# A perceiver kernel: who adds up the exponentials of the second attention

## The chip, the cores and the metric

One core of one Trainium2 chip runs the whole program in one launch. The time is device microseconds of that core, the median of several runs. Five engines work side by side, each with an instruction queue of its own: TensorE (PE in the profile, with its weight loads as PEld), VectorE (DVE), ScalarE (ACT), GpSimd (POOL) and the queue that issues most DMAs (SP). They wait for one another through semaphores only.

## The reference

The program is two layers on 512 latent rows of 512 numbers: a cross attention against 8192 context rows, a scan, experts, a second cross attention against the same context, a linear attention, and a causal attention with experts. The second cross attention, of 16 heads of 32 numbers, is the one that is touched. With q, k and v made before it:

```
for each head h:                       # q: 512 x 32, k and v: 8192 x 32
    s   = (q_h @ k_h.T) * scale        # 512 x 8192
    e   = exp(s - rowmax(s))
    att = (e @ v_h) / e.sum(-1)        # the divisor is the "den" of the names below
out = x + concat(att) @ Wo.T + bo
```

Everything is float32.

## The kernel before

`cross_attention` (L563) serves both cross attentions; `masked` tells the first (with a mask) from the second. The 8192 keys of a head are 64 blocks of 128 keys, taken as 32 pairs, here called steps 0 to 31. A block's scores lie transposed, 128 keys by 512 queries, in a bank of PSUM, so that a sum over keys is a sum over partitions and over tiles.

What each engine issues in a step is fixed by its own loop over `g` (head and step):

- TensorE: `scores` of the first block (L746), `maxima` (L708, two matmuls that give the scores of a later head, 36 steps ahead, for its row maxima), `scores` of the second block, and at every even step a `wave` (L757): the exponentials of four blocks times v, four matmuls in four column groups of 32. Each f32 matmul of a wave runs in two passes, so a wave shows as 8 matmul records. At step 18 (`OUT_STEP`) comes `head_out` of the head before (L783 to L787), at step 29 four small transposes of the maxima (L727).
- ScalarE: two exponentials per step (L861), from PSUM into one of 16 tiles `prob` of 128 x 2 x 512 (two of them lie in the tensor `xnT`), written again 16 steps later, once `tile_free` says that both the wave and the sum are done with the tile.
- VectorE: one `reduce_max` per step over two banks (L927), which frees those banks for the `maxima` two steps on; at step 19 `den_sum` (L967, L969), at step 27 `top_of_rows` (L941), at step 30 `m_lo_rows` (L946). In heads 4, 8 and 12 it also has eight reciprocals (L973), one each at steps 20 to 27.
- GpSimd: adds most `prob` tiles into `den_pool` (L1039 for the first two, L1045 for the others, 128 x 1024 each), and issues the DMAs that add some of the tiles into `den_dma` (L1027, L1031). At step 3 it issues `merge`, a DMA that adds `den_dma` of the head before into `den_pool` (L1021).

The class `Sums` says who sums which tile. Before, in heads 0 to 14 of the second attention: TensorE takes waves 9, 10 and 11, which are tiles 18 to 23, by multiplying them with a matrix of ones (`sum_wave`, L770, four matmuls per wave, issued right behind the wave, into a bank of their own); DMAs take tiles 2, 5, 8, 11, 14, 17, 24, 27 and 30; GpSimd takes the other 17. ScalarE then copies the bank into `den_pe` (`take_sums`, L880), and `head_out` sums `den_pe` over partitions with a matmul of ones (L783). Head 15 has a list of its own (waves 9 to 15 on TensorE).

`Banks` plans the PSUM banks. Three of them (0, 1 and 7) go round between the blocks of scores; "out" (the result of `head_out`) takes one of the three for some steps, and "sums" takes one from step 20 until after step 24, so that the blocks have two left. TensorE may write a block once ScalarE has read the block that was in its bank.

The first attention gives its first five tiles of each head to VectorE, in whole tiles (L957, L960), and GpSimd's first add of the head waits for them.

Of the kernel before, what the change touches and what calls it, by code (L numbers as in the profile page):

```python
# [5 lines left out]
F32 = mybir.dt.float32  # L6
# [4 lines left out]
ALU = mybir.AluOpType  # L11
# [3 lines left out]
P = 128  # L15
T = 512
# [4 lines left out]
H = 16  # L21
DH = D // H
# [395 lines left out]
PAIRS = KT // 2  # L418
# [8 lines left out]
def wave_step(w):  # L427

    return 2 * w + 2
# [39 lines left out]
class Sums:  # L469
# [1 line left out]

    def __init__(self, by_dve, waves, by_dma, last_waves, last_by_dma):
        self.by_dve, self.waves, self.last_waves = by_dve, waves, last_waves
        self.dma_tiles, self.last_dma_tiles = by_dma, last_by_dma
        self.dve_adds = max(0, len(by_dve) - 1)
        self.first_two = 0 if by_dve else 1
        self.pool_adds = len(self.by_pool(0)) - self.first_two

    def pe_waves(self, h):
        return self.waves if h + 1 < H else self.last_waves

    def by_dma(self, h):
        return self.dma_tiles if h + 1 < H else self.last_dma_tiles

    def by_pool(self, h):
        return [p for p in range(PAIRS) if p not in self.by_dve and p not in self.by_dma(h) and p // 2 not in self.pe_waves(h)]

    def pe_done(self, h, w):  # L490

        return len(self.waves) * h + self.pe_waves(h).index(w) + 1

    def dma_done(self, h, p, n_dma):

# [67 lines left out]
def cross_attention(k, ctx, q_hi_lo, k_hi_lo, v_heads, wo, w_out, x_rows, comb, scale, masks, attT):  # L563
# [8 lines left out]
    n_q, n_p = 3, 7 if masked else 16  # L572
    kring = 22 if masked else 36
    if masked:
        sums = Sums([0, 1, 2, 3, 4], [], list(range(5, PAIRS - 2, 3)), [12, 13, 14, 15], [5, 8, 11, 14, 17, 20, 23])
    else:
        sums = Sums([], [9, 10, 11], [2, 5, 8, 11, 14, 17, 24, 27, 30], [9, 10, 11, 12, 13, 14, 15], [2, 5, 8, 11, 14, 17])
    banks = Banks((0, 1, 7), 7, sums)
    q_stack = [k.sbuf(ctx, "q_stack", [QROWS + 2, T], F32R) for _ in range(n_q)]
    k_ring = k.sbuf(ctx, "k_ring", [QROWS + 2, kring, KC], F32R)  # L580
# [9 lines left out]
    den_pe = prob[(PAIRS * (H - 1) + 24) % n_p][:, 0, :] if not sums.waves else k.sbuf(ctx, "den_pe", [P, T], F32)[:]  # L590
# [10 lines left out]
    s_top, s_topT, s_mhi, s_mlo = k.sem("s_top"), k.sem("s_top_turned"), k.sem("s_m_hi"), k.sem("s_m_lo")  # L601
    s_score, s_exp, s_wave = k.sem("s_score"), k.sem("s_exp"), k.sem("s_wave")
    s_pre = k.sem("s_mask_first")
    s_ddve, s_dpool, s_dsum = k.sem("s_den_dve"), k.sem("s_den_pool"), k.sem("s_den_sum")
    s_ddma = [k.sem("s_den_dma", keep=True) for _ in range(n_dma)]
    s_merge = k.sem("s_den_merged", keep=True)
# [11 lines left out]
    def bank_of(kind, n):  # L618
        return k.bank(banks.bank[kind, n])

    def pe_sums(h):

        return h + 1 if sums.waves else int(h + 1 == H)

    def wait_for_bank(e, kind, n):

        if banks.user_before[kind, n] is None:
            return
        kind, n = banks.user_before[kind, n]
        if kind == "block":  # L630
            e.wait_ge(s_exp, n + 1)
        elif kind == "out":
            e.wait_ge(s_dsum, n + 1)
        elif kind == "sums":
            e.wait_ge(s_pesum, pe_sums(n))
        else:
            e.wait_ge(s_mlo, n + 1)

# [8 lines left out]
    with nc.Block() as block:  # L647
# [47 lines left out]
        def _(e):  # L695
# [79 lines left out]
            def head_out(h):  # L775

                out = bank_of("out", h)
                e.wait_ge(s_osb, h + 1)
                wait_for_bank(e, "out", h)
                e.wait_ge(s_merge, 16 * (h + 1))  # L780
                if sums.pe_waves(h):
                    e.wait_ge(s_pesum, pe_sums(h))
# [53 lines left out]
        @block.scalar  # L836
        def _(e):
            def m_hi_rows(h):
                e.wait_ge(s_topT, h + 1)
                e.activation(q_stack[h % n_q][rows_m, :], bank_of("rows", h)[rows_m, :], ACT.Copy).then_inc(s_mhi, 1)  # L840

            def tile_free(g):

                if g < n_p:
                    return
                e.wait_ge(s_wave, waves_done(g - n_p))
                h, p = divmod(g - n_p, PAIRS)
                if p // 2 in sums.pe_waves(h):
                    e.wait_ge(s_sumw, sums.pe_done(h, p // 2))
                elif p in sums.by_dve:  # L850
                    e.wait_ge(s_ddve, sums.dve_done(h, p))
                elif p in sums.by_dma(h):
                    e.wait_ge(s_ddma[h % n_dma], 16 * sums.dma_done(h, p, n_dma))
                else:
                    e.wait_ge(s_dpool, sums.pool_done(h, p))

            def exponentials(b):
                e.wait_ge(s_score, b + 1)
                if b % 2 == 0:
                    tile_free(b // 2)  # L860
                e.activation(prob[b // 2 % n_p][:, b % 2, :], bank_of("block", b), ACT.Exp, scale=scale  # L861
                             ).then_inc(s_exp, 1)

            def mask_first(b):

                wait_for_bank(e, "block", b)
                e.activation(bank_of("block", b), masks[1][:, b % KT, :], ACT.Copy, scale=BIG).then_inc(s_pre, 1)  # L867

            def take_values(h):
                e.wait_ge(s_wave, WAVES * (h + 1))  # L870
                if h > 0:
                    e.wait_ge(s_head, h)
                e.activation(o_sb[:], vbank, ACT.Copy).then_inc(s_osb, 1)

            def take_sums(h):

                if h > 0:
                    e.wait_ge(s_head, h)
                e.wait_ge(s_sumw, sums.pe_done(h, sums.pe_waves(h)[-1]))
                e.activation(den_pe, bank_of("sums", h), ACT.Copy, scale=1.0 / DH).then_inc(s_pesum, 1)  # L880

            def head_rows(h):
                g = slice(DH * (h % 4), DH * (h % 4) + DH)
                e.wait_ge(s_head, h + 1)
                out = bank_of("out", h)
                e.activation(attT[g, h // 4, :], out[0:DH, :], ACT.Copy).then_inc(s_att, 1)
                if h % 4 == 0 and h > 0:
                    e.wait_ge(s_div, h // 4)
                e.activation(den4[g, :], out[DH:2 * DH, :], ACT.Copy).then_inc(s_att, 1)

            if masked:
                for q in range(PAIRS):
                    c2, i = divmod(q, TT)
                    a = turned_banks(q)[0]
                    e.wait_ge(s_maskT, q + 1)
                    e.activation(masks[0][:, i, 2 * c2 * KC:2 * (c2 + 1) * KC],
                                 k.psum[:, a:a + 2, :].rearrange("p b n -> p (b n)"), ACT.Copy).then_inc(s_maskq, 1)
            m_hi_rows(0)
            for g in range(H * PAIRS):
                h, p = divmod(g, PAIRS)  # L900
                exponentials(2 * g)
                if masked and g % 2 == 0:
                    mask_first(2 * g + 2)
                if p == wave_step(WAVES - 1) - PAIRS + 1 and h > 0:
                    take_values(h - 1)
                if p == PAIRS - 2 and h + 1 < H:
                    m_hi_rows(h + 1)
                exponentials(2 * g + 1)
                if p == OUT_STEP and h > 0:
                    head_rows(h - 1)  # L910
                if h + 1 < H and sums.waves and p == wave_step(sums.waves[-1]):
                    take_sums(h)
            take_values(H - 1)
            take_sums(H - 1)
            head_rows(H - 1)

        @block.vector
        def _(e):
# [30 lines left out]
            def add_tile(h, j):  # L949
# [8 lines left out]
                else:  # L958
                    e.wait_ge(s_ddve, sums.dve_adds * h + j)
                    e.tensor_tensor(den[:], den[:], tile, ALU.add).then_inc(s_ddve, 1)  # L960

            def den_sum(h):
                g = slice(DH * (h % 4), DH * (h % 4) + DH)
                e.wait_ge(s_att, 2 * h + 2)
                out = bank_of("out", h)
                if sums.pe_waves(h):
                    e.tensor_tensor(den4[g, :], den4[g, :], out[3 * DH:4 * DH, :], ALU.add).then_inc(s_dhalf, 1)  # L967
                    e.wait_ge(s_dhalf, pe_sums(h))
# [13 lines left out]
            for g in range(H * PAIRS):  # L982
# [2264 lines left out]
```

## Time and profile before

| | |
|---|---|
| median of 3 runs | 4158.3 us (4152.01 to 4160.54) |
| span of the profiled execution | 4154.8 us |
| TensorE busy | 3803.5 us, 92% |
| VectorE busy | 2806.4 us, 68% |
| ScalarE busy | 2342.3 us, 56% |
| GpSimd busy | 1867.7 us, 45% |
| first exponential of the second attention | 2452.5 us |
| last exponential of the second attention | 3343.3 us |

A time line of 40 slices gives the busy share of each engine in tenths, and with it TensorE's granted clock. The second attention is slices 24 to 33:

```profile
PE   7998999999999975789999779999999988769998
DVE  4332877777777268946888667777777453568888
ACT  2222777777777734423777426666666630437775
POOL 0000487887878719910000148888888810000001
PEclk9998999999999987989999969999999997789999
```

Read a time line by columns: a column in which one engine stands at 9 and the others lower is a stage which that engine sets, unless it only looks busy while it waits. Shares over the whole span say little here, since the stages differ.

### The profile page before, as it was taken

How to read it: one execution, taken by the hardware profiler on the slowest of the kernel's cores; microseconds unless marked ns; L12 is line 12 of the kernel's file. 1: busy time of each engine (PE TensorE's matmuls, PEld its weight loads, DVE VectorE, ACT ScalarE, POOL GpSimd, SP SyncE). 2: the span in 40 equal slices, each digit the busy share in tenths (PEclk: the TensorE clock that was granted, in tenths of full speed). 3: DMA queues.
4: the chain of work that ended last, by engine and by line, in shares of the span. 5: the costliest groups of instructions: out<-in, count | busy, mean ns of one | idle time of the engine just before them, and what ended most of it. 6: DMA issues, size and time to landing. Idle time of an engine off the chain costs nothing. (4 is left out here: it accounts for less than half of the span.)

```text
span 4154.8 us, 51637 instructions
## 1 busy us (share of the span) xinstructions
PE 3803.5 (92%) x17986; PEld 2240.3 (54%) x17986; DVE 2806.4 (68%) x3506; ACT 2342.3 (56%) x3654; POOL 1867.7 (45%) x1116
## 2 busy tenths in 40 slices
PE   7998999999999975789999779999999988769998
PEld 6886444444444342257888534444444435447886
DVE  4332877777777268946888667777777453568888
ACT  2222777777777734423777426666666630437775
POOL 0000487887878719910000148888888810000001
PEclk9998999999999987989999969999999997789999
DMA  8996576666666521023888657777777531218887
GB/s 309 332 341 235 123 159 153 154 155 152 156 154 151 126 81 56 0 96 132 320 321 323 239 143 172 175 173 170 171 174 173 126 79 52 61 52 325 322 319 268
DMA packets 295660, 750.49 MB, mean 181 GB/s; under 512 B 55630, under 2 KB 89166, under 8 KB 260842
## 3 DMA queue, kind: packets, MB, share of 16 engines
q1 hardware_dynamic: 246522, 570.48, 41.3%
q0 software_dynamic: 48880, 176.71, 21.4%
q8 instruction: 145, 2.38, 0.2%
q14 instruction: 113, 0.93, 0.1%
HBM read 476.62 MB, written 98.96 MB: 139 GB/s over the span
## 5 line engine op out<-in xcount | busy, mean ns | idle before, releaser
L861 ACT ACTIVATE prob<-psum 128x512 f32<-128x512 f32 x1628 | 917.7, 598 | 397.4 <-PE psum L746 365.0
L1045 POOL TENSOR_TENSOR den_pool<-den_pool,prob 128x1024 f32<-128x1024 f32 x405 | 1021.5, 2522 | 83.0 <-DVE den_pool L960 31.9
L746 PE MATMUL psum<-q_stack,k_ring 98*128 98x512 f32 x2048 | 958.9, 499 | 19.9 <-ACT prob L861 16.6
L931 DVE CUSTOM_DVE_ANT_0 psum<-psum,mask_q 128x1024 f32<-128x1024 f32 x512 | 627.4, 1235 | 240.2 <-PE psum L708 224.3
L927 DVE TENSOR_REDUCE row_max<-psum 128x1 f32<-128x1024 f32 x512 | 609.6, 1220 | 242.1 <-PE psum L708 237.7
L708 PE MATMUL psum<-k_ring,q_stack 96*128 96x512 f32 x2048 | 670.1, 410 | 35.2 <-DMA k_ring<-k_lo 18.4
L746 PEld LDWEIGHTS psum<-q_stack,k_ring 98*128 98x128 f32 x2048 | 394.8, 193 | 523.8 <-ACT psum L867 199.2
L1868 DVE TENSOR_TENSOR weight_lo<-weight_raw,weight_hi 128x2048 fp32r<-128x2048 f32 x180 | 411.4, 2290 | 113.9 <-ACT weight_hi L1864 113.7
L757 PE MATMUL psum<-prob,x 128*32 128x512 f32 x3256 | 472.9, 605 | 2.9 <-ACT prob L861 0.8
L708 PEld LDWEIGHTS psum<-k_ring,q_stack 96*128 96x128 f32 x2048 | 390.9, 195 | 122.8 <-issue 34.6
L2043 POOL DMA_DIRECT2D y_slots<-xnT x28 | 15.4, 550 | 860.6 <-ACT xnT L2147 860.6
L1864 ACT ACTIVATE weight_hi<-weight_raw 128x2048 fp32r<-128x2048 f32 x180 | 343.1, 1916 | 18.1 <-DMA weight_raw<-in_L_ffn_w 7.8
L745 PE MATMUL psum<-mask_k,ident_big 128*128 128x512 fp8e4 x768 | 301.3, 392 | 11.8 <-ACT prob L861 8.2
L861 ACT ACTIVATE xnT<-psum 128x512 f32<-128x512 f32 x420 | 244.2, 597 | 106.0 <-PE psum L746 100.1
L1045 POOL TENSOR_TENSOR den_pool<-den_pool,xnT 128x1024 f32<-128x1024 f32 x112 | 287.6, 2568 | 19.6 <-DVE den_pool L960 13.6
L1027 POOL DMA_DIRECT2D den_dma<-prob x184 | 160.9, 875 | 106.6 <-ACT prob L861 63.3
L1512 PE MATMUL psum<-dB_u,ident 128*128 128x512 f32 x256 | 138.6, 685 | 70.5 <-POOL dB_u L1443 57.4
L103 PE MATMUL psum<-weight_hi,hidden_T_hi 128*128 128x512 f32 x480 | 196.7, 410 | 3.8 <-DVE weight_lo L1868 3.6
L745 PEld LDWEIGHTS psum<-mask_k,ident_big 128*128 128x128 bf16 x768 | 74.7, 97 | 218.5 <-ACT prob L861 99.7
L103 PE MATMUL psum<-weight_hi,hidden_T_lo 128*128 128x512 f32 x480 | 189.0, 394 | 0.0
L103 PE MATMUL psum<-weight_lo,hidden_T_hi 128*128 128x512 f32 x480 | 188.7, 393 | 0.0
L2135 ACT ACTIVATE xnT<-psum 128x512 f32<-128x512 f32 x120 | 71.8, 599 | 151.0 <-PE psum L103 150.7
(459 smaller groups left out, 6616.0 us busy)
## 6 DMA issues: line engine op xcount, KB each, us to landing
den_dma<-prob POOLq DMA_DIRECT2D x211, 512.0 KB, 5.0
k_ring<-k_hi SPq DMA_DIRECT2D x1024, 64.0 KB, 2.3
weight_raw<-in_L_ffn_Wu SPq DMA_DIRECT2D x60, 1024.0 KB, 7.1
weight_raw<-in_L_ffn_Wd SPq DMA_DIRECT2D x60, 1024.0 KB, 5.3
weight_raw<-in_L_ffn_w SPq DMA_DIRECT2D x60, 1024.0 KB, 6.6
den_dma<-xnT POOLq DMA_DIRECT2D x72, 512.0 KB, 5.0
k_ring<-k_lo SPq DMA_DIRECT2D x512, 64.0 KB, 2.6
w_o<-in_L_ffn_w SPq DMA_DIRECT2D x30, 1024.0 KB, 7.2
```

Source lines behind the costliest of these rows:

```text
L103: ins = e.matmul(out, lhsT, rhs, start=start and n == 0, stop=stop and n == len(terms) - 1)
L708: ins = e.matmul(max_banks(q)[:, a * KC:(a + 1) * KC], q_stack[h % n_q][0:QROWS, i * P:(i + 1) * P], k_ring[0:QROWS, (n + a) % kring, :], ...
L745: e.matmul(out, k.ident_big[:], masks[1][:, t, :], start=True, stop=False)
L746: e.matmul(out, k_ring[:, n % kring, kt * P:(kt + 1) * P], q_stack[h % n_q][:], start=not masked, stop=True, skip_group_check=masked and b ...
L757: ins = e.matmul(vbank[n * DH:(n + 1) * DH, :], v_buf[t // 16][:, t % 16 * DH:(t % 16 + 1) * DH], prob[(PAIRS * h + t // 2) % n_p][:, t % ...
L861: e.activation(prob[b // 2 % n_p][:, b % 2, :], bank_of("block", b), ACT.Exp, scale=scale).then_inc(s_exp, 1)
L927: e.reduce_max(out, max_banks(q), AXIS_X).then_inc(s_red, 1)
L931: e.tensor_tensor_reduce(out=max_banks(q), in0=max_banks(q), in1=masks[0][:, i, 2 * c2 * KC:2 * (c2 + 1) * KC], scale=1.0, scalar=-3.0e38, ...
L1027: e.dma_start(den_dma[h % n_dma][:], tile, accum_op=ALU.add).then_inc(s_ddma[h % n_dma], 16)
L1045: e.tensor_tensor(den[:], den[:], tile, ALU.add).then_inc(s_dpool, 1)
L1864: e.activation(self.hi[q % RING][:], self.raw[q % RAW][:], ACT.Copy).then_inc(self.s_whi, 1)
L1868: e.tensor_tensor(self.lo[q % RING][:], self.raw[q % RAW][:], self.hi[q % RING][:].bitcast(F32), ALU.subtract).then_inc(self.s_wlo, 1)
```

## The change

It replaces the three sum waves of heads 0 to 14 of the second attention. Tiles 3, 8, 13, 18, 23 and 28 now go to VectorE, which adds them in halves of 128 x 512 into one of two tiles `den_dve`: the first add takes both halves of tile 3, and each of the other five tiles has an add for either half, 11 adds per head. They are issued behind the reduction of steps 5, 10, 11, 15, 16, 20, 21, 25, 26, 30 and 31. `head_out` multiplies `den_dve` with ones where it took `den_pe`. The "sums" bank and `take_sums` stay for head 15 alone. DMAs take tiles 1, 4, 7, 10, 14, 17, 20, 24 and 27, nine as before, and GpSimd again the other 17. `tile_free` waits for VectorE's count where a tile is one of the six. The first attention is as it was.

```diff
@@ class Sums
     def pe_waves(self, h):
-        return self.waves if h + 1 < H else self.last_waves
+        return [] if h + 1 < H else self.last_waves
+
+    def by_halves(self, h):
+        return self.halves if h + 1 < H else []
+    def half_adds(self, h):
+        return 2 * len(self.by_halves(h)) - 1
+    def half_steps(self, h):
+        ops = [(self.halves[0] + 2, 0, None)] if self.by_halves(h) else []
+        for n, p in enumerate(self.by_halves(h)[1:], 1):
+            ops += [(p + 2, n, 0), (p + 3, n, 1)]
+        return ops
...
@@ def cross_attention
-        sums = Sums([], [9, 10, 11], [2, 5, 8, 11, 14, 17, 24, 27, 30], [9, 10, 11, 12, 13, 14, 15], [2, 5, 8, 11, 14, 17])
+        sums = Sums([], [3, 8, 13, 18, 23, 28], [1, 4, 7, 10, 14, 17, 20, 24, 27], [9, 10, 11, 12, 13, 14, 15],
+                    [2, 5, 8, 11, 14, 17])
+    den_dve = [k.sbuf(ctx, "den_dve", [P, T], F32) for _ in range(2 if sums.halves else 0)]
...
@@ TensorE, head_out
+                elif sums.by_halves(h):
+                    e.wait_ge(s_dvhalf, sums.half_adds(h) * (h + 1))
+                    e.matmul(out[3 * DH:4 * DH, :], k.ones[:, 0:DH], den_dve[h % 2][:], start=True, stop=True)
...
@@ ScalarE
+                elif p in sums.by_halves(h):
+                    e.wait_ge(s_dvhalf, sums.half_done(h, p))
...
-                if h + 1 < H and sums.waves and p == wave_step(sums.waves[-1]):
-                    take_sums(h)
...
@@ VectorE
+            def add_half(h, j, n, half):
+                p, den = sums.halves[n], den_dve[h % 2][:]
+                tile = prob[(PAIRS * h + p) % n_p]
+                e.wait_ge(s_exp, 2 * (PAIRS * h + p) + 2)
+                if j == 0:
+                    if h >= 2:
+                        e.wait_ge(s_head, h - 1)
+                    e.tensor_tensor(den, tile[:, 0, :], tile[:, 1, :], ALU.add).then_inc(s_dvhalf, 1)
+                else:
+                    e.wait_ge(s_dvhalf, sums.half_adds(h) * h + j)
+                    e.tensor_tensor(den, den, tile[:, half, :], ALU.add).then_inc(s_dvhalf, 1)
...
+                for j, (step, n, half) in enumerate(sums.half_steps(h)):
+                    if step == p:
+                        add_half(h, j, n, half)
                 if p == OUT_STEP + 1 and h > 0:
                     den_sum(h - 1)
```

## Rows read from the trace of the kernel before

**Rows 1.** Busy time by stretch, each about one head: us, busy us (instructions) of each engine, clock.

```profile
core 0: us, PE busy (x) PEld busy (x) DVE busy (x) ACT busy (x) POOL busy (x), PEclk, DMA share, GB/s
2564.00:2620.00 56.00, 54.94 (x300) 26.62 (x296) 40.62 (x38) 38.19 (x70) 46.53 (x27) 1.00 0.77 173
```

**Rows 2.** One line of ScalarE (one instance per head), first and last start.

```profile
L873 ACT ACTIVATE o_sb<-psum x5: 591/592/592, 2621.7 to 2845.5; 128x512 f32<-128x512 f32 x5
```

**Rows 3.** TensorE in order of time, steps 18 to 27 of a head: start us, us, instruction.

```profile
2763.26 0.50 PE L746 MATMUL psum<-q_stack,k_ring 98*128 98x512 f32 x1 [0.82 <-ACT prob L861]
...
2764.39 1.06 PE L757 MATMUL psum<-prob,x 128*32 128x512 f32 x8
2765.28 1.04 PE L770 MATMUL psum<-prob,ones 128*32 128x512 f32 x8
2766.25 0.50 PE L746 MATMUL psum<-q_stack,k_ring 98*128 98x512 f32 x1
2766.59 0.63 PE L708 MATMUL psum<-k_ring,q_stack 96*128 96x512 f32 x2
...
2770.43 0.50 PE L746 MATMUL psum<-q_stack,k_ring 98*128 98x512 f32 x1
...
2774.61 0.50 PE L746 MATMUL psum<-q_stack,k_ring 98*128 98x512 f32 x1
...
2778.05 0.50 PE L746 MATMUL psum<-q_stack,k_ring 98*128 98x512 f32 x1
2778.39 0.64 PE L708 MATMUL psum<-k_ring,q_stack 96*128 96x512 f32 x2
...
2779.33 0.63 PE L708 MATMUL psum<-k_ring,q_stack 96*128 96x512 f32 x2
2779.80 0.40 PE L746 MATMUL psum<-q_stack,k_ring 98*128 98x512 f32 x1
2780.13 1.07 PE L757 MATMUL psum<-prob,x 128*32 128x512 f32 x8
2781.13 0.50 PE L746 MATMUL psum<-q_stack,k_ring 98*128 98x512 f32 x1
```

**Rows 4.** VectorE in order of time, steps without extra work, then a head with reciprocals.

```profile
2755.23 2.35 DVE L927 TENSOR_REDUCE row_max<-psum 128x1 f32<-128x1024 f32 x2 [0.72 <-PE psum L708]
2758.31 2.35 DVE L927 TENSOR_REDUCE row_max<-psum 128x1 f32<-128x1024 f32 x2 [0.72 <-PE psum L708]
...
2720.80 0.54 DVE L973 RECIPROCAL den_of_heads<-den_of_heads 128x64 f32<-128x64 f32 x1
2721.26 1.16 DVE L927 TENSOR_REDUCE row_max<-psum 128x1 f32<-128x1024 f32 x1
```

**Rows 5.** Lines of VectorE by source, last the first attention's adds: ns min/median/max.

```profile
L967 DVE TENSOR_TENSOR den_of_heads<-den_of_heads,psum x15: 687/691/696, 2539.7 to 3317.7; 32x512 f32<-32x512 f32 x15
L946 DVE SCALAR_TENSOR_TENSOR q_stack<-q_stack,lo_sign,psum x15: 755/757/758, 2505.7 to 3287.9; 2x512 fp32r<-2x512 f32 x15
L960 DVE TENSOR_TENSOR den_pool<-den_pool,prob x35: 1215/1221/1225, 460.4 to 1399.3; 128x1024 f32<-128x1024 f32 x35
```

**Rows 6.** GpSimd by source, then VectorE in order of time, end of the first attention.

```profile
L1045 POOL TENSOR_TENSOR den_pool<-den_pool,prob x2: 2701/2952/3202, 1390.8 to 1393.6; 128x1024 f32<-128x1024 f32 x2
...
1393.17 1.38 DVE L957 TENSOR_TENSOR den_pool<-prob,xnT 128x1024 f32<-128x1024 f32 x1 [4.50 <-ACT xnT L861]
1394.66 3.23 DVE L960 TENSOR_TENSOR den_pool<-den_pool,xnT 128x1024 f32<-128x1024 f32 x1
1397.99 2.55 DVE L960 TENSOR_TENSOR den_pool<-den_pool,prob 128x1024 f32<-128x1024 f32 x2
```

**Rows 7.** GpSimd by source, adds of the second attention: ns min/median/max.

```profile
L1045 POOL TENSOR_TENSOR den_pool<-den_pool,prob x194: 2362/2391/3074, 2499.3 to 3324.6; 128x1024 f32<-128x1024 f32 x194
```

**Rows 8.** Waits of 2500 to 3300 us: engine line, waited for, us in total, times, longest.

```profile
DVE row_max L927 <- PE psum L708: 200.1, 222, 1.8
POOL den_dma L1027 <- ACT prob L861: 61.8, 35, 5.7
POOL den_dma L1027 <- DMA den_dma<-prob: 22.7, 5, 4.8
```

More of the change, by code:

```diff
@@ L469, with __init__ @@
 class Sums:
-    def __init__(self, by_dve, waves, by_dma, last_waves, last_by_dma):
-        self.by_dve, self.waves, self.last_waves = by_dve, waves, last_waves
+    def __init__(self, by_dve, halves, by_dma, last_waves, last_by_dma):
+        self.by_dve, self.halves, self.last_waves = by_dve, halves, last_waves
         self.dma_tiles, self.last_dma_tiles = by_dma, last_by_dma
@@ L481, in pe_waves, with third, half_done @@
     def pe_waves(self, h):
-        return self.waves if h + 1 < H else self.last_waves
+        return [] if h + 1 < H else self.last_waves
+    def by_halves(self, h):
+        return self.halves if h + 1 < H else []
+    def third(self, h):
+        return bool(self.pe_waves(h) or self.by_halves(h))
+    def half_adds(self, h):
[5 more added lines that the diff above has]
+        return ops
+    def half_done(self, h, p):
+        return self.half_adds(0) * h + 2 * self.halves.index(p) + 1
     def by_dma(self, h):
@@ L487, in by_pool @@
     def by_pool(self, h):
-        return [p for p in range(PAIRS) if p not in self.by_dve and p not in self.by_dma(h) and p // 2 not in self.pe_waves(h)]
+        return [p for p in range(PAIRS) if p not in self.by_dve and p not in self.by_dma(h)
+                and p // 2 not in self.pe_waves(h) and p not in self.by_halves(h)]
     def pe_done(self, h, w):
-        return len(self.waves) * h + self.pe_waves(h).index(w) + 1
+        return self.pe_waves(h).index(w) + 1
     def dma_done(self, h, p, n_dma):
@@ L588, in cross_attention @@
     den_dma = [k.sbuf(ctx, "den_dma", [P, 2, T], F32) for _ in range(n_dma)]
-    den_pe = prob[(PAIRS * (H - 1) + 24) % n_p][:, 0, :] if not sums.waves else k.sbuf(ctx, "den_pe", [P, T], F32)[:]
+    den_pe = prob[(PAIRS * (H - 1) + 24) % n_p][:, 0, :] if not sums.halves else k.sbuf(ctx, "den_pe", [P, T], F32)[:]
+    den_dve = [k.sbuf(ctx, "den_dve", [P, T], F32) for _ in range(2 if sums.halves else 0)]
     den4 = k.sbuf(ctx, "den_of_4_heads", [P, T], F32)
@@ L603, in cross_attention @@
     s_pre = k.sem("s_mask_first")
+    s_dvhalf = k.sem("s_den_dve_half")
     s_ddve, s_dpool, s_dsum = k.sem("s_den_dve"), k.sem("s_den_pool"), k.sem("s_den_sum")
@@ L619, in bank_of, with thirds @@
         return k.bank(banks.bank[kind, n])
-    def pe_sums(h):
-        return h + 1 if sums.waves else int(h + 1 == H)
+    def thirds(h):
+        return sum(sums.third(n) for n in range(h + 1))
     def wait_for_bank(e, kind, n):
@@ L634, in wait_for_bank @@
         elif kind == "sums":
-            e.wait_ge(s_pesum, pe_sums(n))
+            e.wait_ge(s_pesum, 1)
         else:
@@ L781, in head_out @@
                 if sums.pe_waves(h):
-                    e.wait_ge(s_pesum, pe_sums(h))
+                    e.wait_ge(s_pesum, 1)
                     e.matmul(out[3 * DH:4 * DH, :], k.ones[:, 0:DH], den_pe, start=True, stop=True)
+                elif sums.by_halves(h):
+                    e.wait_ge(s_dvhalf, sums.half_adds(h) * (h + 1))
+                    e.matmul(out[3 * DH:4 * DH, :], k.ones[:, 0:DH], den_dve[h % 2][:], start=True, stop=True)
                 e.matmul(out[0:DH, :], comb, o_sb[:], start=True, stop=True)
@@ L965, in den_sum @@
                 out = bank_of("out", h)
-                if sums.pe_waves(h):
+                if sums.third(h):
                     e.tensor_tensor(den4[g, :], den4[g, :], out[3 * DH:4 * DH, :], ALU.add).then_inc(s_dhalf, 1)
-                    e.wait_ge(s_dhalf, pe_sums(h))
+                    e.wait_ge(s_dhalf, thirds(h))
                 e.tensor_tensor(den4[g, :], den4[g, :], out[2 * DH:3 * DH, :], ALU.add).then_inc(s_dsum, 1)
```

## The prediction

> **What bounds the kernel now.** I read the time line of slices first: in the second attention TensorE stands at 9 in nearly every slice, VectorE at 7, ScalarE at 6 and GpSimd at 8. One head closer [rows 1]: in 56.0 us TensorE is busy 54.9, VectorE 40.6, ScalarE 38.2, GpSimd 46.5, at a granted clock of 1.00, which is 2.4 GHz. Head follows head every (2845.5 - 2621.7) / 4 = 55.95 us [rows 2]. The waits say the same: VectorE waits for TensorE's maxima [rows 8], hardly the reverse. So TensorE's queue sets the head, and whatever leaves it shortens the head until another queue is full. The order of time shows a head's cadence: two steps (four scores, four maxima, one wave) start 3.08 us apart, 2778.05 to 2781.13, while with a sum wave they take 4.18, 2766.25 to 2770.43 and 2770.43 to 2774.61 [rows 3].
>
> **What goes.** The first sum wave: wave starts at 2764.39 and sum wave at 2765.28, the next score at 2766.25; without a sum wave the score comes 1.00 after its wave (2780.13 to 2781.13). So 1.86 - 1.00 = 0.86 us. Then 4.18 - 3.08 = 1.10 for each of the next two sum waves, 0.87 of it the matmuls and the rest a wait for ScalarE while the blocks have two banks instead of three, and 2778.05 - 2774.61 - 3.08 = 0.36 for `take_sums` and the bank's last steps. In sum 3.42 us per head [rows 3], for 15 heads 51 us. A head would be 55.95 - 3.42 = 52.5 us. `head_out` keeps four products, `den_dve` in the place of `den_pe`. The 0.82 us in which TensorE waits for ScalarE at step 20 stays: the "out" bank and ScalarE's two copies are as before [rows 3]. ScalarE loses 0.6 us of 38 per head and stays hidden.
>
> **What GpSimd and the DMAs get.** Counts are equal, 17 tiles and 9 tiles. Only places move. GpSimd's 46.5 us [rows 1] fit in 52.5. What before gave GpSimd rest, the stretch with tiles 18 to 23 off its list (most of its 61.8 us waiting for exponentials [rows 8]), is spread over the head. DMA tiles stand three steps apart at the closest, as before, and waits for landings were 22.7 us in 14 heads on a queue that has slack [rows 8]. I cost this at nothing; the cover is GpSimd's 6 us of slack per head, and the 16 tiles of `prob`. If that were gone, each us that GpSimd is over 52.5 would lengthen the head by one.
>
> **What VectorE gets, without any contention.** The trace has no half add between two tiles of SBUF. Nearest: a whole tile takes 1221 ns, an add of 512 columns with one input in PSUM 691 [rows 5]. Subtract what overlaps with the next instruction: a reciprocal of 0.54 gives way after 0.46 (2720.80 to 2721.26) [rows 4], so 0.69 - 0.08 = 0.61 us per half add. Eleven make 6.7, and VectorE's head becomes 40.6 + 6.7 = 47.3 of 52.5 us. It fits on the whole; what matters is when. In two plain steps VectorE has 0.72 us free [rows 4]. How late may it be before TensorE waits? The maxima of the two steps start 0.34 and 1.28 into the 3.08 us [rows 3]. The first reduction starts 0.68 behind its matmuls and lasts 1.13, to 2.15; its banks are wanted at 3.42: 1.2 us to spare. The second ends at 3.4 and is wanted at 4.36: 1.0 us. Two half adds (1.22) against 0.72 + 1.0: no wait. The semaphores that a half add waits for are old by then (its exponentials are two steps back, and `tile_free` looks 16 steps back), so as such they hold up nothing.
>
> **What VectorE gets with GpSimd in its way.** This decides. GpSimd is in an add for 16 x 2.39 = 38 us of each head [rows 1, 7]. In the first attention VectorE's whole-tile adds never meet one of GpSimd's, since that one waits for them, but once, at its end [rows 6]. GpSimd starts an add at about 1393.6 that takes 3202 ns instead of 2391: VectorE's add from 1393.17 was under way, to 1394.55. VectorE's next add starts at 1394.66 and takes 3.23 us instead of 1.22: it ends 1.1 after GpSimd's end at 1396.8, one whole add's time. Either one stands still until the other is through. VectorE's reductions, from PSUM, show nothing of the kind (2.35 for two, 0.72 apart, beside GpSimd's adds) [rows 4]. So a half add, with both inputs in SBUF, should wait for the rest of whatever add GpSimd is in, and the reduction behind it in VectorE's queue waits too, and behind that TensorE's `maxima`, and behind that the scores.
>
> The Trainium skill ("SBUF — State Buffer", section "Who interferes with whom") has this as a rule: a VectorE instruction with two SBUF inputs contends with a GpSimd instruction that reads SBUF, and the later one stands until the earlier is done; it also says that one with at most one SBUF input does not. The trace agrees with the 3.23 beside 1.22 us, for one meeting [rows 6]. By this rule all 165 half adds are exposed; if that one meeting were chance, none would be, and the sum would be the first rival's.
>
> The price: a head will be near 60 us, so a half add meets GpSimd's add with chance 38 / 60 = 0.64, and half of 2.39 is left then: 0.77 us on average. The bounds are 0 and 2.39 for a wait; the observed one is 3.23 - 1.22 = 2.01. I take the average, as the phases of the two queues drift. A half add then costs 0.61 + 0.77 = 1.38.
> - Five pairs of half adds (steps 10 and 11, 15 and 16, 20 and 21, 25 and 26, 30 and 31): 2.76 - 0.72 - 1.0 = 1.04 each, 5.2 us that TensorE waits.
> - The lone one at step 5: 1.38 - 1.2 = 0.2 on average, but a wait of up to 2.39 overshoots more than a short one gives back: 0.4.
> - At steps 19 and 30 `den_sum` (two of 0.69) and `m_lo_rows` (0.76) [rows 5] have already used the free 0.72 ahead of the half adds: 2 x 0.75 = 1.5.
> Together 7.1 us per head, less the 3.4 saved: +3.7, for 15 heads +55. In heads 4, 8 and 12 eight reciprocals of 0.46 (3.7 us) fall in steps 20 to 27, until now covered by the slower steps of the sum waves; some 2.8 of it comes out: 3 x 2.8 = 8. GpSimd loses up to 0.6 per half add, 6.7 per head: 53 us of 60, still hidden. Sum: +63 us. On the profiled span, 4154.8 + 63 = 4218; the median of the runs lies 3.5 above that span, so 4221 us. Given the mechanism, 4170 to 4260: the low end if the waits average 0.4, the high end if 1.0.
>
> **Rivals.**
> (1) GpSimd and VectorE don't hold each other up, or hardly: faster. Only the 6.7 us per head count; the pairs at steps 20 and 30 come out with some 0.2 each, the reciprocals with 2.5 in three heads: -51 + 15 x 0.2 + 8 = -40, so 4118, or 4107 if even these hide. For it: only one meeting is on record, the added instruction is half as long, and VectorE has 15 us free. Against: both engines lengthened in that meeting, each by what the other had left. It decides from a mean wait under about 0.25 us, where the stalls in TensorE are below 3.4 per head.
> (2) Break-even: waits happen, but TensorE's lead and VectorE's idle time from step 0 to 9 take them up, so that VectorE's own sum is the limit: 40.6 + 6.7 + 11 x 0.77 = 55.8 us, against 55.95 before: 4158 within a few us. Against: a lead of 1.0 us cannot carry 2.76 us of work from steps 10 and 11 to step 9.
> (3) Worse: the second half add of a pair comes one reduction (1.1 us) after the first, when GpSimd has just started its next add, so that it waits 2.39 - 1.1 = 1.3 nearly always, and GpSimd, held up in turn, frees tiles late: 0.5 us more in each of five pairs, 15 x 2.5 = 38 on top: 4260.
>
> **Chances.** Forecast 0.62, (1) 0.20, (2) 0.08, (3) 0.10. A difference under 0.2%, 8 us, can't be told from none in these runs. Faster takes (1) and a little of the others: 0.20; same: 0.06; slower: 0.74. The range for all: 4112 to 4255, which leaves out the lowest part of (1) and the upper half of (3).
>
> **What would show it.** The half adds (128 x 512, two SBUF inputs) with a minimum near 0.69 us and many at 1 to 3 us: forecast; all at 0.69: rival (1). GpSimd's adds with more above 2.7 us. Waits of TensorE's `maxima` for `row_max`, now next to nothing, at some 7 us per head, behind the steps with half adds. TensorE's share below 90% of the stretch, VectorE's "busy" (a blocked add counts) well above 47 per head. The head at 59 to 61 us instead of 55.95; plain steps without half adds (6 to 9) still at 3.08 per two; steps 20 to 25 no longer at 4.18. I'd be wrong if half adds find GpSimd between adds more often than its busy time says, or if the lock, once TensorE is late, settles in a phase where the two miss each other.

## The result

The changed kernel takes 4354.32 us (median of 4 runs, 4344.4 to 4380.61) against 4155.16 us for the kernel before: a ratio of 1.0488, 95% interval 1.0455 to 1.0522, slower by about 199 us. The profiled execution has a span of 4378.9 us, 224 above that of before; it is the longest of the four.

The time line of the changed kernel, 40 slices of its span as before; the second attention is slices 23 to 33:

```profile
PE   7998999999999767899997888888888889769998
DVE  4334777777775479568885889988888834377888
POOL 0000678888888279200002367766666640000001
PEclk9998999999999878899998789988899888789999
```

VectorE is up from 7 to 8 and 9, TensorE down to 8, GpSimd down from 8 to 6 and 7, and the granted clock, 9 before in every slice of the second attention but its first, is 7 to 9. The same in numbers, each kernel in the stretch 2500 to 3300 us. The columns are us, then busy us and instructions of TensorE, its weight loads, VectorE, ScalarE and GpSimd, then clock, DMA share, GB/s. The kernel before, then the changed one:

```profile
2500.00:3300.00 800.00, 783.27 (x4223) 377.79 (x4221) 579.46 (x546) 547.18 (x992) 670.48 (x377) 1.00 0.75 169
```

```profile
2500.00:3300.00 800.00, 681.21 (x3080) 317.89 (x3078) 691.99 (x560) 430.57 (x769) 542.13 (x297) 0.89 0.61 137
```

The head, once per head as in [rows 2], is (3516.8 - 2525.5) / 14 = 70.8 us instead of 55.95. The changed kernel's line of ScalarE, then VectorE's two lines of half adds, ns min/median/max:

```profile
L904 ACT ACTIVATE o_sb<-psum x15: 591/592/593, 2525.5 to 3516.8; 128x512 f32<-128x512 f32 x15
...
L999 DVE TENSOR_TENSOR den_dve<-prob x15: 2584/2697/2715, 2466.5 to 3457.7; 128x512 f32<-128x512 f32 x15
...
L1002 DVE TENSOR_TENSOR den_dve<-den_dve,prob x150: 676/1745/3287, 2475.5 to 3515.6; 128x512 f32<-128x512 f32 x150
```

The shortest is 0.68 us. The first add of a head takes 2.6 to 2.7 every time, the others 1.9 on average; over all, (287.2 + 40.4) / 165 = 1.99 us. Of the 165, 150 start while GpSimd is inside an add, and 17 take less than 0.75 us. What one of them does, around the add of step 5 in one head, in order of time by engine:

```profile
2743.40 1.22 DVE L956 TENSOR_REDUCE row_max<-psum 128x1 f32<-128x1024 f32 x1 [0.72 <-PE psum L734]
2744.54 2.70 DVE L999 TENSOR_TENSOR den_dve<-prob 128x512 f32<-128x512 f32 x1
2747.16 3.47 DVE L956 TENSOR_REDUCE row_max<-psum 128x1 f32<-128x1024 f32 x3
...
2744.31 5.14 POOL L1090 TENSOR_TENSOR den_pool<-den_pool,prob 128x1024 f32<-128x1024 f32 x2 [1.03 <-ACT prob L892]
...
2746.27 0.63 PE L772 MATMUL psum<-q_stack,k_ring 98*128 98x512 f32 x2
2748.52 0.70 PE L734 MATMUL psum<-k_ring,q_stack 96*128 96x512 f32 x2 [1.61 <-DVE row_max L956]
2749.05 0.39 PE L772 MATMUL psum<-q_stack,k_ring 98*128 98x512 f32 x1
2749.37 1.94 PE L783 MATMUL psum<-prob,x 128*32 128x512 f32 x8
2751.24 0.80 PE L772 MATMUL psum<-q_stack,k_ring 98*128 98x512 f32 x1
```

GpSimd starts an add at 2744.31, the first of two, which ends near 2746.7 if it takes its usual 2.39 us. VectorE's half add starts 0.23 us later and ends at 2747.24, some 0.5 us behind that. No semaphore of the program stands between the two adds, so for this pair of engines the opening's sentence, that they wait for one another through semaphores only, does not hold. The reductions behind it are late, and TensorE stands 1.61 us for `row_max`. Then its wave takes 1.94 us instead of 1.07 [rows 3]. The clock in two short stretches, the wait and the wave, says why the wave is slow:

```profile
2746.90:2748.50 1.60, 0.00 (x1) 0.01 (x1) 1.60 (x3) 0.89 (x2) 1.60 (x1) 1.00 1.09 242
2749.30:2751.30 2.00, 2.00 (x10) 0.27 (x9) 1.33 (x2) 0.60 (x1) 0.48 (x2) 0.51 0.76 239
```

0.51 is the lower of the clock's levels, 1.2 GHz, in a stretch that starts 0.8 us after the end of TensorE's wait. GpSimd's adds kept their median, 2393 ns against 2391 [rows 7]: it was nearly always there first.

### The profile page after: what moved, and what is told of

Its sections match the earlier page's. It is cut to its first block and busy times, and to the rows that moved or that the text cites. A ratio compares the mean times of both kernels' runs of the same rounds, so it can differ in the third digit from the quotient of the medians.

```text
span 4378.9 us, 51218 instructions
## 1 busy us (share of the span) xinstructions
PE 3886.3 (89%) x17626; PEld 2263.1 (52%) x17626; DVE 3109.6 (71%) x3671; ACT 2338.8 (53%) x3639; POOL 1884.4 (43%) x1116
## 5 line engine op out<-in xcount | busy, mean ns | idle before, releaser
L1090 POOL TENSOR_TENSOR den_pool<-den_pool,prob 128x1024 f32<-128x1024 f32 x390 | 978.5, 2509 | 246.7 <-ACT prob L892 188.5
L772 PE MATMUL psum<-q_stack,k_ring 98*128 98x512 f32 x2048 | 976.9, 511 | 17.9 <-ACT prob L892 16.0
L734 PE MATMUL psum<-k_ring,q_stack 96*128 96x512 f32 x2048 | 709.1, 430 | 175.9 <-DVE row_max L956 147.0
L772 PEld LDWEIGHTS psum<-q_stack,k_ring 98*128 98x128 f32 x2048 | 412.5, 202 | 547.9 <-ACT psum L898 200.8
L734 PEld LDWEIGHTS psum<-k_ring,q_stack 96*128 96x128 f32 x2048 | 402.8, 205 | 303.9 <-issue 122.3
L783 PE MATMUL psum<-prob,x 128*32 128x512 f32 x3256 | 514.2, 659 | 1.3 <-ACT prob L892 0.8
L1090 POOL TENSOR_TENSOR den_pool<-den_pool,xnT 128x1024 f32<-128x1024 f32 x127 | 318.9, 2511 | 50.6 <-ACT xnT L892 29.6
L892 ACT ACTIVATE xnT<-psum 128x512 f32<-128x512 f32 x420 | 245.9, 597 | 151.0 <-PE psum L772 147.2
L1002 DVE TENSOR_TENSOR den_dve<-den_dve,prob 128x512 f32<-128x512 f32 x150 | 287.2, 1915 | 0.9
L1072 POOL DMA_DIRECT2D den_dma<-prob x199 | 172.8, 868 | 68.4 <-ACT prob L892 47.6
L1557 PE MATMUL psum<-dB_u,ident 128*128 128x512 f32 x256 | 138.5, 685 | 70.7 <-POOL dB_u L1488 57.6
```

The costliest lines, as they stand in the source:

```text
L734: ins = e.matmul(max_banks(q)[:, a * KC:(a + 1) * KC], q_stack[h % n_q][0:QROWS, i * P:(i + 1) * P], k_ring[0:QROWS, (n + a) % kring, :], ...
L772: e.matmul(out, k_ring[:, n % kring, kt * P:(kt + 1) * P], q_stack[h % n_q][:], start=not masked, stop=True, skip_group_check=masked and b ...
L783: ins = e.matmul(vbank[n * DH:(n + 1) * DH, :], v_buf[t // 16][:, t % 16 * DH:(t % 16 + 1) * DH], prob[(PAIRS * h + t // 2) % n_p][:, t % ...
L1002: e.tensor_tensor(den, den, tile[:, half, :], ALU.add).then_inc(s_dvhalf, 1)
L1090: e.tensor_tensor(den[:], den[:], tile, ALU.add).then_inc(s_dpool, 1)
```

## The experiments

Ratios are to the kernel before, with 95% intervals. All edits touch only the second attention: e3, e4, e9, e10, e12 and e14 all of its heads, the others heads 0 to 14. e1, e2, e3, e4, e5, e7, e8, e11, e12 and e13 are edits of the changed kernel; e6, e9, e10 and e14 are edits of the kernel before. Diffs show the main lines, with ... for the rest.

**e1.** No half adds:

```diff
-                for j, (step, n, half) in enumerate(sums.half_steps(h)):
-                    if step == p:
-                        add_half(h, j, n, half)
...
```

> The kernel after without its 11 half adds per head (tiles 3, 8, 13, 18, 23, 28 of heads 0 to 14 are left out of the divisor; den_dve is set to ones once). It measures what leaving TensorE's sum waves is worth alone. Theory A (my step 'what goes': 3.4 us per head leave TensorE's queue, which alone sets the head): 51 us below before, 4104, a head of 52.5 us, granted clock 1.00 in the second attention. Rival B (TensorE's queue isn't the only bound; ScalarE, GpSimd or the moved DMA tiles hold the head): between 4130 and 4160.

Measured: 4152.31 us, ratio 0.9988 (0.9978 to 0.9997). The time is that of rival B, the first heads are those of theory A. e1's line of ScalarE, the first five heads and the last ten:

```profile
L903 ACT ACTIVATE o_sb<-psum x5: 592/592/592, 2508.4 to 2718.4; 128x512 f32<-128x512 f32 x5
...
L903 ACT ACTIVATE o_sb<-psum x10: 590/591/593, 2774.4 to 3283.5; 128x512 f32<-128x512 f32 x10
```

The first five heads are 210.0 / 4 = 52.5 us apart, the forecast number, the later ones 509.1 / 9 = 56.6. GpSimd's queue in a later head:

```profile
2978.73 0.87 POOL L1071 DMA_DIRECT2D den_dma<-prob  x1 [1.76 <-ACT prob L891]
2979.32 2.70 POOL L1089 TENSOR_TENSOR den_pool<-den_pool,prob 128x1024 f32<-128x1024 f32 x1
2985.47 0.86 POOL L1071 DMA_DIRECT2D den_dma<-prob  x1 [3.44 <-DMA den_dma<-prob]
```

Where one add alone stands between two DMAs that add into the same tile, the second waits for the first to land: 3.44 us here. In the stretch 2500 to 3300 us such waits are 70.7 us, and ScalarE, which writes the `prob` tiles again, waits for those landings too, and then TensorE for ScalarE (engine line, waited for, us in total, times, longest):

```profile
POOL den_dma L1071 <- DMA den_dma<-prob: 70.7, 31, 4.1
ACT prob L891 <- DMA den_dma<-prob: 82.1, 52, 3.2
PE psum L772 <- ACT prob L891: 29.9, 37, 2.0
```

The new list of DMA tiles has that at tiles 1 and 4 (one add between), 7 and 10, 17 and 20; the old one had two adds, or the six steps of the sum waves, between nearly all.

**e2.** Half adds with one SBUF input:

```diff
-                    e.tensor_tensor(den, den, tile[:, half, :], ALU.add).then_inc(s_dvhalf, 1)
+                    e.reduce_max(half_max[:, j:j + 1], tile[:, half, :], AXIS_X).then_inc(s_dvhalf, 1)
...
```

> The kernel after with every half add turned into a maximum over the same 512 columns of the same half tile, at the same place in VectorE's queue, with the same semaphores: one SBUF input instead of two, about the same length (0.6 to 0.7 us). The six tiles are so left out of the divisor. Theory A (two SBUF inputs collide with GpSimd's adds): each takes about 0.7 us, TensorE hardly waits for row_max, clock 1.00, 4104 to 4120. Rival B (VectorE is simply given too much, at the wrong steps): the time stays near 4354, at least above 4250.

Measured: 4150.43 us, 0.9983 (0.9973 to 0.9994), the same as e1 without any. The 165 instructions take 668 to 689 ns. So VectorE's extra work as such, at these steps, costs nothing beside e1's own limit, which is also why the time is not theory A's 4104 to 4120. Rival B falls. The edit takes away two things at once, the second SBUF input and the 512 columns that a half add writes to SBUF. That it is the input, a line of VectorE in the changed kernel shows: it has one SBUF input and one in PSUM, and writes 512 columns to SBUF, in 32 partitions.

```profile
L1011 DVE TENSOR_TENSOR den_of_heads<-den_of_heads,psum x15: 681/684/687, 2571.5 to 3543.6; 32x512 f32<-32x512 f32 x15
```

Of these 15, 14 lie wholly inside one of GpSimd's adds, and none is longer for it.

**e3.** GpSimd writes only:

```diff
-                e.tensor_tensor(den[:], den[:], tile, ALU.add).then_inc(s_dpool, 1)
+                if masked:
+                    e.tensor_tensor(den[:], den[:], tile, ALU.add).then_inc(s_dpool, 1)
+                else:
+                    e.memset(den[:], 1.0).then_inc(s_dpool, 1)
```

> The kernel after, with GpSimd's adds of the second attention (all but the first of each head) turned into a memset of den_pool: they write but read nothing; the divisor is so left without GpSimd's tiles. The half adds are untouched, two SBUF inputs. Theory A (they wait for GpSimd's reads): half adds of 0.69 us (some longer beside the one add per head that stays), 4104 to 4125. Rival C (the wait is for the write side or for anything GpSimd runs): half adds stay above 1 us, though the memsets are shorter, and the time stays above 4180.

Measured: 4119.4 us, 0.9911 (0.9893 to 0.993), as theory A has it; rival C falls. The untouched half adds are back at 0.68 us, a little over half of the 1.22 of a whole tile [rows 5]:

```profile
L1002 DVE TENSOR_TENSOR den_dve<-den_dve,prob x150: 674/681/2046, 2471.6 to 3249.3; 128x512 f32<-128x512 f32 x150
```

Of the 165 half adds only the one of 2.05 us is above 0.8, and GpSimd had started a multiplication that reads SBUF 0.13 us ahead of it. The edit also makes GpSimd's instructions shorter (1.10 us on average, busy 376.20 of 800 us where it was 542.13), but 86 of the half adds overlap one of its memsets, and all but that one stay below 0.8 us.

**e4, e12.** Needless matmuls where TensorE stands waiting, four at each place, then two:

```diff
+FILL_STEPS, FILLS = (0, 1, 7, 13, 17, 18, 23, 27, 28), 4
...
+                    filler(h, p)
                     maxima(g + PAIRS + LEAD)
...
```

> The kernel after plus 36 needless score matmuls per head of the second attention: four copies of the step's second score, ahead of the maxima, at steps 0, 1, 7, 13, 17, 18, 23, 27 and 28, where TensorE stands waiting for row_max. They are 36 x 0.23 = 8.3 us of work per head at 2.4 GHz and change no result. Theory D (over half of the loss, some 130 of 224 us of the profiled run, is TensorE at 1.2 GHz after its waits): the waits are filled, the granted clock of the stretch goes from 0.89 to above 0.97, and the kernel gets faster though it does more: 4230 to 4290. Rival E (the clock has no part in it, the waits alone cost): the same or slower, 4354 to 4480.

> e4 with two needless matmuls at each of the nine places instead of four. Theory D (the clock falls when TensorE stands still for long): the gaps are left longer, clock between the kernel after's 0.89 and e4's 0.99, 4290 to 4330. If the filler's own work were what is left of the loss: faster than e4's 4294 by up to 60.

Measured: e4 4294.25 us, 1.0329 (1.0312 to 1.0346), 4 us above the range of theory D; e12 4322.57, 1.0387 (1.0368 to 1.0406), inside its own. More work on the engine that sets the head, and the kernel is 60 us faster than without; half the filler gives about half of it, 32. The stretch 2500 to 3300 of e4, then of e12:

```profile
2500.00:3300.00 800.00, 753.16 (x3776) 402.10 (x3778) 734.51 (x614) 465.47 (x833) 587.70 (x321) 0.99 0.66 148
```

```profile
2500.00:3300.00 800.00, 716.00 (x3411) 356.41 (x3410) 716.57 (x579) 447.54 (x799) 563.81 (x309) 0.94 0.63 143
```

The clock is 0.89, 0.94, 0.99 with no, two and four of them. The 150 half adds behind the first of a head average 1.89 us in e12 and 1.82 in e4, where they had 1.92: nearly unchanged in e12, 15 us less in e4 over all 150, which may be a part of its gain. So rival E falls and the clock is a cause of its own: holding it brings some 60 us back beyond what the filler costs, which is not known.

**e5.** e1 with another list of DMA tiles:

```diff
-        sums = Sums([], [3, 8, 13, 18, 23, 28], [1, 4, 7, 10, 14, 17, 20, 24, 27], [9, 10, 11, 12, 13, 14, 15],
+        sums = Sums([], [3, 8, 13, 18, 23, 28], [0, 4, 7, 11, 15, 19, 22, 26, 30], [9, 10, 11, 12, 13, 14, 15],
```

> e1 (no half adds, the six tiles left out of the divisor) with one list changed: the nine DMA tiles of a head are 0, 4, 7, 11, 15, 19, 22, 26, 30 instead of 1, 4, 7, 10, 14, 17, 20, 24, 27, so that GpSimd has two adds between any two DMAs but the first two. In e1 the first five heads took 52.5 us, as forecast, and the later ones 56 to 57, with GpSimd waiting 2 to 4 us for a DMA landing wherever one add alone stood between two DMAs. Theory F (those waits fill GpSimd's queue, the backlog reaches ScalarE's tile_free after five heads, and that is where e1's 51 us went): 52.5 to 53 us in all heads, 4104 to 4115. Rival G (GpSimd's adds themselves are too many for 52.5 us): heads of 55 or more later on, above 4135.

Measured: 4106.07 us, 0.9878 (0.9863 to 0.9892), theory F; GpSimd's waits for landings fell from 70.7 to 28.8 us, ScalarE's from 82.1 to none, and the heads are even, (3293.9 - 2508.1) / 15 = 52.4 us:

```profile
L903 ACT ACTIVATE o_sb<-psum x16: 591/592/598, 2508.1 to 3293.9; 128x512 f32<-128x512 f32 x16
```

Some 49 us is what the sum waves are worth (51 forecast), and 46 of them e1 lost to the order of one list.

**e6, e10.** The kernel before with two sum waves, then also a later merge (the last two lines of the diff are e10's alone):

```diff
-        sums = Sums([], [9, 10, 11], [2, 5, 8, 11, 14, 17, 24, 27, 30], ...
+        sums = Sums([], [10, 11], [0, 3, 6, 9, 12, 15, 18, 25, 28, 31], ...
...
-    n_dma, merge_step = (1, 1) if masked else (2, 3)
+    n_dma, merge_step = (1, 1) if masked else (2, 6)
```

> The kernel before with two sum waves (10 and 11) instead of three; tiles 18 and 19 go one to GpSimd and one to a DMA, and the ten DMA tiles are 0, 3, 6, 9, 12, 15, 18, 25, 28, 31. Computes all of the reference. Theory F (GpSimd can take 17 adds if two stand between DMAs): one sum wave less is 1.1 us per head, 54.9 instead of 55.95, 16 us in all: 4142 beside 4158. Rival G (GpSimd is full at about 56 us per head anyway): 4155 to 4190.

> e6 (two sum waves, 18 tiles on GpSimd, ten on DMAs) with the merge DMA issued at step 6 instead of 3. In e6 the first five heads took 54.9 us and the later ones 57 to 60, and GpSimd waited 1.8 us per head at the merge for the landing of tile 31's DMA. Theory F: that wait goes, GpSimd's queue shortens by it, 4155 to 4175. If GpSimd's 17 adds are simply too many: 4180 as e6.

Measured: 4184.53 us, 1.0067 (1.0055 to 1.0079), and 4185.24, 1.0066 (1.0052 to 1.0079). The first heads of e6 are 54.9 us apart, the later ones 55 to 63. The time of e6 is that of rival G. Why is not shown. e10 took away GpSimd's waits at the merge (25.6 us in e6), but the later merge lands later, and `head_out` waits for it; TensorE in e6, then in e10:

```profile
PE psum L783 <- DMA den_pool<-den_dma: 6.0, 6, 2.0
```

```profile
PE psum L783 <- DMA den_pool<-den_dma: 25.3, 9, 5.2
```

So e10 does not acquit the merge, and that 17 adds and ten DMAs are too much for GpSimd stays the likely reading only.

**e7.** Half adds of tiles 3, 13 and 23 only:

```diff
-            ops += [(p + 2, n, 0), (p + 3, n, 1)]
+            if n in (2, 4):
+                ops += [(p + 2, n, 0), (p + 3, n, 1)]
...
```

> The kernel after with 5 of its 11 half adds per head: those of tiles 3, 13 and 23 (steps 5, 15, 16, 25, 26); tiles 8, 18 and 28 are left out of the divisor. Theory A with D (each meeting costs TensorE its wait and then its clock): about half of the 200 us between e1 and the kernel after go, 4230 to 4270, with half adds still near 1.9 us on average. Rival B' (a threshold in VectorE's sum of work: with 5 adds it has room again): below 4190.

Measured: 4190.93 us, 1.0073 (1.0059 to 1.0088), 39 us below the range of the first theory and 1 us above the second's: neither has it. Above e1, 5 adds cost 39 us and 11 cost 202: 0.5 and 1.2 us per add and head, though the single adds are no shorter (2.20 us on average, in a profiled execution that is the slowest of the five, 4226.54 us). The loss grows faster than the count. That fits with e1's own heads, already held up by GpSimd, hiding part of the first waits; it was not taken apart further.

**e8, e11.** Half adds ahead of the step's reduction, then with e5's list as well:

```diff
                 h, p = divmod(g, PAIRS)
+                for j, (step, n, half) in enumerate(sums.half_steps(h)):
+                    if step == p:
+                        add_half(h, j, n, half)
                 if g + PAIRS + LEAD < H * PAIRS:
                     maxima(g + PAIRS + LEAD)
...
-                for j, (step, n, half) in enumerate(sums.half_steps(h)):
-                    if step == p:
-                        add_half(h, j, n, half)
```

> The kernel after with each half add issued ahead of its step's reduction instead of behind it; the same instructions, all of the reference computed. In the trace of the kernel after the first add of a head takes 2.58 to 2.71 us every time, since GpSimd's add starts 0.2 us before it. Theory H (the phases are locked, not drifting: GpSimd starts when ScalarE's exponentials are done and VectorE's half add comes just behind): 1.1 us earlier VectorE mostly gets in first, the mean half add falls from 1.92 to below 1.3 us, the clock rises above 0.95, 4180 to 4260. Rival I (phases drift, the wait is an average over GpSimd's busy share): mean half add 1.7 to 2.0 us, 4330 to 4380.

> e8 (half adds ahead of the reductions) with e5's list of DMA tiles (0, 4, 7, 11, 15, 19, 22, 26, 30). Computes all of the reference. If GpSimd's queue has a share in the loss of the kernel after: 4220 to 4245. If only the meetings matter: within 25 us of e8's 4270, either way, as another order of GpSimd's work meets the half adds at other moments.

Measured: e8 4270.48 us, 1.0261 (1.0241 to 1.0281), 84 us faster than the changed kernel by a move of one loop, and 10 above the range of theory H; e11 4310.82, 1.039 (1.0351 to 1.043), 40 slower than e8 and outside both of its ranges. The first add of a head in e8:

```profile
L999 DVE TENSOR_TENSOR den_dve<-prob x15: 680/682/692, 2460.2 to 3349.3; 128x512 f32<-128x512 f32 x15
```

All 15 went from 2.7 to 0.68 us. The other 150 average 1.66 us, so that the mean of all is 1.57, above the 1.3 of theory H and below the 1.7 of rival I. Only some of the meetings are broken up: 54 of the 165 half adds take less than 0.75 us, where it was 17. With e5's order of GpSimd's queue it is 40 (e11, mean 1.79), so there are more meetings again. In e8 TensorE also waits 18.1 us for `q_stack`, which VectorE now writes behind a half add; in the changed kernel it had no such wait.

**e13.** e2 with e5's list; e13's diff is those two.

> e2 (half adds turned into maxima with one SBUF input, the six tiles left out of the divisor) with e5's list of DMA tiles. It has all of the kernel after's VectorE work at the same steps, no meetings, and a GpSimd queue without the lone adds between DMAs. If the meetings are all that VectorE's work costs: 4106 to 4125, e5 and the few us of the reciprocal heads that I forecast (some 2.5 us in three heads). If VectorE's plain work at steps 19 to 31 costs TensorE more than that: 4130 to 4150.

Measured: 4112.87 us, 0.9896 (0.988 to 0.9911). This is in the first of the two ranges. With neither meetings nor lone adds, all of VectorE's new work costs 7 us over e5, and the change's idea would have been worth 46.

**e9, e14.** VectorE's adds kept apart from GpSimd's by a semaphore:

```diff
-        sums = Sums([], [9, 10, 11], [2, 5, 8, 11, 14, 17, 24, 27, 30], ...
+        sums = Sums([0, 1, 2], [10, 11], [3, 6, 9, 12, 15, 18, 25, 28, 31], ...          # e9
+        sums = Sums([0, 1, 2, 3, 4], [11], [5, 8, 11, 14, 17, 20, 25, 28, 31], ...       # e14
-    n_dma, merge_step = (1, 1) if masked else (2, 3)
+    n_dma, merge_step = (1, 1) if masked else (2, 6)
```

> From the kernel before: two sum waves (10, 11) instead of three; tiles 0, 1 and 2 of a head are added by VectorE in whole tiles at steps 3 and 4, as the first attention does it, and GpSimd's first add of the head waits for them, so that the two never meet; DMAs take 3, 6, 9, 12, 15, 18, 25, 28, 31, the merge is issued at step 6. Computes all of the reference. If it is the meetings with GpSimd that make VectorE's adds dear: two adds of 1.22 us each, TensorE's head 54.9 us plus a stall of at most 0.5, GpSimd with 16 adds as before: 4140 to 4152. If VectorE's adds are dear anyway, or GpSimd's wait for them (some 3 us per head) fills its queue: above 4160.

> e9 taken further: one sum wave (11), tiles 0 to 4 on VectorE in whole tiles at steps 3 to 6, GpSimd's first add waits for them, DMAs take 5, 8, 11, 14, 17, 20, 25, 28, 31. Computes all of the reference. TensorE's head would be 53.8 us; four adds of 1.14 in four steps against 0.36 us free per step and about 1 us of lead leave a stall of 2.1: 55.9, about e9's 55.7, if GpSimd's 16 adds and its wait of some 4 us fit. 4150 to 4165. Clearly below 4150 if VectorE can run later than I think; above 4170 if GpSimd is full.

Measured: e9 4151.7 us, 0.9985 (0.9976 to 0.9994); e14 4162.86, 1.001 (1.0001 to 1.0019). One head of e9, VectorE then GpSimd:

```profile
2737.02 1.23 DVE L957 TENSOR_TENSOR den_pool<-prob 128x1024 f32<-128x1024 f32 x1
2738.16 1.22 DVE L927 TENSOR_REDUCE row_max<-psum 128x1 f32<-128x1024 f32 x1
2739.30 1.22 DVE L960 TENSOR_TENSOR den_pool<-den_pool,prob 128x1024 f32<-128x1024 f32 x1
...
2740.66 4.88 POOL L1045 TENSOR_TENSOR den_pool<-den_pool,prob 128x1024 f32<-128x1024 f32 x2 [3.21 <-DVE den_pool L960]
```

GpSimd starts when VectorE is done, and whole tiles with two SBUF inputs take their 1.22 us, in all heads but the last, where one takes 3.21. e9 computes all of the reference and is the only such version here faster than the kernel before, by 0.15%, which is at the edge of what can be told. Taken further (e14) nothing is left. TensorE's waits for `row_max` go from 2.3 us in e9 to 19.0 in the same 800 us, 1.2 us more per head, where the sum wave that is gone gives 1.1.

## Why the prediction was wrong

It had the direction and one of two mechanisms, and a third of the size: +63 us forecast, with 4255 us as the end of its range, +199 and 4354 measured. It gave no price to TensorE's lower clock behind the waits, and that is the step that failed most. Step by step, per head, of the profiled executions:

- **What goes**, 3.4 us: right. e5 gives 52.4 for the head where I had 52.5.
- **What GpSimd and the DMAs get**, "I cost this at nothing": wrong, though in the changed kernel it cannot show, since its heads are 70 us long. It shows in e1: 46 us, nearly the whole gain of the sum waves. I compared busy time, 46.5 of 52.5, and left out the waits inside its queue. The row was there: 22.7 us of waits for landings [rows 8], which I dismissed with the old order of the list in mind; I wrote that the closest DMAs are three steps apart as before, and did not count the adds between them.
- **What VectorE gets without contention**, 0.61 us a half add that mostly hides: right (e2, e13; 7 us in all where rival 1 had 11).
- **With GpSimd in its way**: right in kind, shown by e2 and e3 from both sides. By the Trainium skill ("SBUF — State Buffer", "Who interferes with whom") a GpSimd instruction that only writes does not contend with a two-input VectorE one; e3 agrees, with 681 ns at the median.
- **The price**, "0.77 us on average ... as the phases of the two queues drift": wrong. The half adds average 1.99 us where 0.69 + 0.77 = 1.46 was forecast, a wait of 1.30. I took the chance of a meeting as 0.64; 150 of 165 start inside an add of GpSimd's, 0.91. The phases don't drift. GpSimd, now with slack, starts its add when the exponentials are done, and VectorE's half add comes 0.2 us behind at step 5, every time; e8 moves it, and that wait is gone. The other places repeat from head to head too: the one at step 20 takes 0.68 or 0.69 in 14 of 15 heads, the one at step 31 is 1.60 to 1.63 in 14 of 15. Rival 3 had locked phases, and its wait of 1.3 for the second add of a pair measures 1.20; but the first adds of the pairs wait as long, 1.25, and its price of 38 us had no clock in it either.
- **The sum per head**, 7.1 + 0.5 us of waiting: TensorE idles (800 - 681.21) / 800 x 70.8 = 10.5 us in the changed kernel against 1.4 of 52.4 in e5: 9.1 more, 137 us over 15 heads where I had 115. Given waits of 1.30, my rule would have said 5 x (2 x 1.91 - 0.72 - 1.0) = 10.5 us for the pairs alone, so it errs high. That these two errors offset each other in part is luck. TensorE's waits in the stretch 2500 to 3300 us, in the changed kernel for `row_max`, in the kernel before for ScalarE:

```profile
PE psum L734 <- DVE row_max L956: 110.5, 79, 2.6
```

```profile
PE psum L746 <- ACT prob L861: 12.2, 17, 0.8
```

- **The clock** is the term that is missing, and the step that failed most. My first paragraph took it at 1.00 and nothing later asked whether it stays. TensorE's busy time per head is 60.3 us against 51.0 in e5, for the same matmuls: 9.3 us, 139 over 15 heads. So waits and busy time give 137 + 139 - 51 = 225, where the two spans differ by 224; this has to close, as a head is idle time plus busy time. How much of the 139 is the clock, the granted clock says: (1.00 - 0.89) x 70.8 = 7.8 us per head, 117 over 15 heads. The other 22 are not explained. They are there at a clock of 0.99 too: in e4 a head is (3430.7 - 2517.5) / 14 = 65.2 us and TensorE is busy 753.16 / 800 x 65.2 = 61.4 us of it, 8.3 of it filler by the estimate in e4's expectation, which leaves 53.1, 2 us more than in e5. Nor are the 117 all gained if the clock is held, as a faster TensorE only meets the late reductions sooner; e4 got some 60 back, net of the filler. The kernel before had shown the lower level just ahead of this attention; I gave it no price. The kernel before, 2400 to 2410 us:

```profile
2400.00:2410.00 10.00, 8.95 (x17) 3.73 (x16) 9.15 (x9) 0.00 (x0) 8.17 (x18) 0.50 0.57 142
```

## What to carry to other kernels

Ahead of giving VectorE an operation with two SBUF inputs, see what GpSimd reads at that moment, and keep the two apart by order or by a semaphore; if they can meet, read from the trace which of the two starts first at each place, as the wait repeats there head after head. An average over GpSimd's busy time said 0.77 us here, and it was 1.30. Count a queue's waits for its own DMAs into its load: two adds between two chained DMAs or one was worth 46 us here. And price a wait put on TensorE for the clock as well: here 79 waits of up to 2.6 us for `row_max`, in 800 us, came with a clock of 0.89, while the 17 waits of at most 0.8 us for ScalarE's exponentials in the kernel before left it at 1.00.

## What the runs showed of the hardware

- TensorE's granted clock fell from 1.00 to 0.51 in the stretch that began 0.8 us after a wait of 1.6 us had ended, and 36 matmuls per head that compute nothing, put where TensorE waited, brought the clock from 0.89 to 0.99 and made the kernel 60 us faster.
- A VectorE add with two SBUF inputs and a GpSimd add that reads SBUF exclude each other for whole instructions: half adds of 0.68 us took up to 3.29. One input instead of two (e2), or a GpSimd that writes only (e3), and they take 0.68 again.
- One reduction (1.1 us) earlier in VectorE's queue turned 2.70 us into 0.68 for the first half add of all 15 heads (e8).
